# A transformer block on one core: the first batch's ranking and maxima beside products, the last batch's second half of tokens first, the next batch's turned tiles in the last group of heads

## The chip, the core and the metric

One core of one Trainium2 chip runs the whole kernel. The metric is the device time of one execution in microseconds (us).

## What is computed

Eight batches (B = 8) of 1024 tokens with 512 features go through three sublayers. `ln` is a layer norm without weights.

```python
def ffn(y):                       # expert-choice routing, 75% of the tokens
    scores = y @ w_router
    top = top_k(scores, 768)      # per batch
    y[top] = gelu(y[top] @ w_block)
    return y
x = x + 0.5 * ffn(ln(x))
h = ln(x)                         # 16 heads of 32, latent width 64, causal
q_lat = (h @ Wq.T) per head @ q_to_latent;  k_lat = h @ Wk_down.T;  v_lat = h @ Wv_down.T
x = x + (softmax(mask(q_lat @ k_lat.T / 8)) @ v_lat @ v_up) @ Wout.T
x = x + 0.5 * ffn(ln(x))
```

## The kernel before, in words

**Events.** `program_order()` (line 100) returns one list of events for the whole kernel. Each engine's program walks this list and emits its own share of every event, so the list is the order of the work on every engine, and on SyncE (SP), which issues the DMAs. Nothing is reordered later: an engine that waits holds up all that follows it. Every product of matrices is made of three passes of high and low parts (`passes`, line 721), so that most results are copied twice: the high part by ScalarE (ACT), the low part, result minus high, by VectorE (DVE).

The events are, with the engines that take part:

- XL, XR, XS, OUT: 1 MB loads, reloads, spills and stores of half a batch of x (SP).
- ST, VA, RS, NM: statistics of a tile of 128 tokens (DVE), variance, its power -0.5 (GpSimd, POOL), scaled mean. NO: the normalized tile (ACT, two slots).
- T: four transposes of a normalized tile (TensorE, PE), high part (ACT), low part (DVE). The first index is 0 for the first feed-forward layer, 1 for attention, 2 for the last layer.
- SD, SM, SC, RT, RF: the ranking of the tokens. SD is the dot product with the router (DVE), SC a row of scores (PE, ACT), RT compares one tile's scores with all 1024 (DVE, two or three instructions), RF makes the selection.
- GX, F, G, CB: scaling of x (POOL), block product (PE), gelu (ACT), the sum into x (DVE).
- LAT, Q, K, V: the projections. WS: splitting a weight into high and low (ACT, DVE).
- S, MX: scores of a unit of 512 columns for two heads, less the row maximum; and the product that finds the row maxima of the next group of four heads (PE, then exp on ACT for S, reductions on DVE for MX). MC, XT: gather and transpose the maxima (DVE, PE), and a DMA of the row (SP, line 570).
- AM: causal mask (POOL). PV, DEN: products with values and with ones (PE). AC, HT, HR, HE: division of the heads (ACT, DVE).
- HS: a quarter of the heads split for the output product (ACT high, POOL low). O: the output product of a tile (PE) and its sum into x (DVE).

**Stages.** Heads come in four groups (g = 0 to 3) of four. `attention(b)` (line 173) gives each group 18 chunks, two for each of the 9 units: chunk 2u holds the first pair of S and MX, chunk 2u + 1 the second. Beside the scores of group g run the maxima of group g + 1, so group 3 has no maxima; there both S pairs of a unit stand in chunk 2u. PV and DEN come two units behind. Into these chunks other work is put: the end of the batch before into group 0, the next batch's statistics into group 1, its eight T of layer 0 with NO into group 2 (lines 265 to 268), its dots, SC, RT, RF, GX and first two F into group 3 (lines 269 to 277). `project(b, left)` (line 134) then holds the other F, the projections and the first maxima of the next batch, and `back(b)` (line 217) the output products and most of the last feed-forward layer.

**First and last batch.** For batch 0, `front(0)` and `project(0, None)` run alone: ranking comes after all weights but one are split (line 140), most maxima stand in `project`, and units 5 and 6 of the maxima with XT stand alone behind it (line 249). For batch 7, the split of the heads (HS) follows all of attention (line 282); then come O in the order of the tiles, and RT, GX, CB and the store.

**PSUM.** `take(ring, first, size, count)` (line 315) gives each result its banks from rings that are walked in the order of the list; a result waits until the last user of its bank is copied away. S and MX beside each other take four banks of ring A (0 to 5); T of layer 0 in later batches takes one bank of the same ring (line 331); group 3's S take ring N (0 to 3); SC and the first F ring F (4 and 5); PV and DEN have banks 6 and 7. The projections and the early maxima share ring H, all eight banks.

Of the kernel before, what the change touches and what calls it, by code (L numbers as in the profile page):

```python
# [99 lines left out]
def program_order():  # L100


    def stats(s, b, i):
# [9 lines left out]
    def front(b):  # L113


        out = []
        for c in range(NC):
            for i in range(TC * c, TC * (c + 1)):
                out += stats(0, b, i)
            out += scales(0, b, c)  # L120
        out += [("NO", 0, b, 0), ("NO", 0, b, 1)]
        for i in range(NT):
# [94 lines left out]
    def back(b):  # L217


        def more(kind, *rest):  # L220
# [831 lines left out]
```

## Time and profile before

| what | value |
|---|---|
| median of 3 runs | 2492.73 us (2490.47 to 2492.91) |
| the profiled execution's own time | 2491.35 us |
| its span | 2489.6 us |
| PE / DVE / ACT / POOL busy | 90% / 73% / 47% / 16% |
| TensorE clock granted, mean | 0.963 of full speed |

The span runs from the first instruction to the last. The share of busy time is a mean over stages: one batch takes about 300 us, and eight of them overlap only in part. Granted clock is 1.00 at 2.4 GHz and 0.50 at 1.2 GHz.

### The profile page before, as it was taken

The page shows a single profiled execution, that of the slowest core. Times are in us where ns is not written, and L with a number is a line of the kernel's source. Part 1 is how long each engine was busy: PE and PEld are TensorE (multiplying, and loading weights), DVE is VectorE, ACT ScalarE, POOL GpSimd, SP SyncE. Part 2 cuts the span into 40 slices and gives each one's busy share as a digit, 9 for nine tenths or more (in the row PEclk, how much of TensorE's full clock was granted, in tenths as well). Part 3 has the DMA queues.
Part 4 walks back from the last instruction along what each step waited for, and adds up shares of the span by engine and source line. Part 5 has one row for each costly group of instructions (what it writes and reads, how often), then busy time and mean ns, then how long its engine had stood idle before and what let it go on. Part 6 is the DMA issues. An engine that isn't in the chain of part 4 may idle for free.

```text
span 2489.6 us, 53117 instructions
## 1 busy us (share of the span) xinstructions
PE 2253.0 (90%) x21504; PEld 1395.5 (56%) x21504; DVE 1807.2 (73%) x5077; ACT 1181.1 (47%) x2070; POOL 395.8 (16%) x510
## 2 busy tenths in 40 slices
PE   5779999999998999999999999989998899988976
PEld 4534477445674556644566446754476445764445
DVE  5668757887678766787667876778757787678726
ACT  3335543465434654446434464345643455434542
POOL 0101211112101121011111102111111112111121
PEclk9879999899999999999999999989999999999988
DMA  3200021100301002010021101120021100301000
GB/s 131 102 1 3 2 84 53 69 2 6 98 35 69 3 19 85 35 69 3 20 83 52 53 2 53 52 74 29 2 78 59 69 3 2 95 8 69 2 2 34
DMA packets 69601, 106.42 MB, mean 43 GB/s; under 512 B 2544, under 2 KB 32752, under 8 KB 67312
## 3 DMA queue, kind: packets, MB, share of 16 engines
q1 hardware_dynamic: 69360, 103.03, 12.2%
q8 instruction: 173, 2.83, 0.5%
q14 instruction: 68, 0.56, 0.1%
HBM read 64.75 MB, written 37.75 MB: 41 GB/s over the span
## 4 chain that ended last, share of the span: by engine, by line
PE 71%; DVE 15%; issue 6%; ACT 6%; POOL 2%; DMA 0%; DVEq 0%; POOLq 0%; ACTq 0%
PE psum L726 27%; PE psum L739 18%; PE psum L839 9%; PE psum L846 7%; DVE psum L984 4%; PE psum L742 4%; ACT pr L706 4%; DVE part L982 3%; PE psum L768 2%; PE psum L753 2%; DVE junk L932 1%; DVE junk L934 1%; DVE nt_l L907 1%; POOL x L604 1%; ACT nt_h L625 1%
## 5 line engine op out<-in xcount | busy, mean ns | idle before, releaser
L706 ACT ACTIVATE pr<-psum 128x512 f32<-128x512 f32 x1152 | 617.7, 596 | 607.3 <-PE psum L742 607.2
L739 PE MATMUL psum<-qk,qk 32*128 32x512 f32 (+3 forms) x4608 | 519.3, 373 | 95.5 <-DVE part L984 41.7
L984 DVE CUSTOM_DVE_ANT_0 psum<-psum,mask_b 128x512 f32<-128x512 f32 (+3 forms) x1024 | 472.4, 521 | 115.9 <-PE psum L753 114.2
L739 PEld LDWEIGHTS psum<-qk,qk 32*128 32x128 f32 x4608 | 326.4, 190 | 403.6 <-DVE part L984 124.2
L753 PE MATMUL psum<-qk,qk 32*128 32x512 f32 (+3 forms) x4608 | 520.5, 376 | 25.5 <-DVE part L982 19.7
L982 DVE TENSOR_REDUCE part<-psum 128x1 f32<-128x512 f32 x512 | 324.8, 680 | 45.9 <-PE psum L753 43.8
L753 PEld LDWEIGHTS psum<-qk,qk 32*128 32x128 f32 x4608 | 318.5, 191 | 50.1 <-DVE part L982 26.1
L839 PE MATMUL psum<-pr,v_sb 128*32 128x512 f32 (+3 forms) x3072 | 316.6, 508 | 1.6 <-ACT ht L625 1.6
L617 POOL TENSOR_SCALAR_AFFINE_SELECT pr<-pr 128x512 f32<-128x512 f32 x256 | 159.2, 641 | 962.2 <-ACT pr L706 962.2
L846 PE MATMUL psum<-pr,ones 128*32 128x512 f32 (+3 forms) x3072 | 312.0, 501 | 0.0
L646 ACT ACTIVATE norm<-x,nmr,rstd 128x512 f32<-128x512 f32 x192 | 152.4, 811 | 173.0 <-DVE nmr L901 173.0
L742 PE MATMUL psum<-mrow,minus 1*128 1x512 f32 (+3 forms) x1536 | 218.5, 349 | 0.0
L907 DVE TENSOR_TENSOR nt_l<-psum,nt_h 128x512 fp32r<-128x512 f32 x192 | 131.0, 686 | 109.3 <-ACT nt_h L625 107.9
L726 PE MATMUL psum<-wb_h,nt_h 128*128 128x512 f32 x512 | 206.9, 404 | 1.8 <-ACT nt_act L670 1.8
L726 PE MATMUL psum<-wb_h,nt_l 128*128 128x512 f32 x512 | 200.6, 392 | 0.0
L726 PE MATMUL psum<-wb_l,nt_h 128*128 128x512 f32 x512 | 200.4, 391 | 0.0
L768 PE MATMUL psum<-ident,norm 128*128 128x128 f32 x768 | 122.7, 288 | 41.3 <-ACT norm L646 31.5
L604 POOL TENSOR_SCALAR x<-x,gain,shift 128x512 f32<-128x512 f32 x128 | 104.7, 837 | 338.6 <-DVE gain L949 338.6
L625 ACT ACTIVATE nt_h<-psum 128x512 fp32r<-128x512 f32 x192 | 114.6, 597 | 84.5 <-PE psum L768 84.4
L846 PEld LDWEIGHTS psum<-pr,ones 128*32 128x32 f32 x3072 | 77.3, 109 | 121.5 <-issue 105.6
L768 PEld LDWEIGHTS psum<-ident,norm 128*128 128x128 f32 x768 | 89.4, 145 | 99.7 <-issue 46.0
L984 DVE DVE_READ_ACCUMULATOR2_ANT part<- 128x1 f32 x1024 | 143.5, 140 | 0.0
(109 smaller groups left out, 3277.6 us busy)
## 6 DMA issues: line engine op xcount, KB each, us to landing
x<-x_dram SPq DMA_DIRECT2D x16, 1024.0 KB, 6.7
spill_x<-x SPq DMA_DIRECT2D x16, 1024.0 KB, 4.7
x<-spill_x SPq DMA_DIRECT2D x16, 1024.0 KB, 7.3
out_dram<-x SPq DMA_DIRECT2D x16, 1024.0 KB, 5.0
w_h<-scratch_o SPq DMA_DIRECT2D x28, 256.0 KB, 3.1
w_l<-scratch_o SPq DMA_DIRECT2D x28, 256.0 KB, 3.3
w_h<-scratch_q SPq DMA_DIRECT2D x6, 1024.0 KB, 4.9
w_l<-scratch_q SPq DMA_DIRECT2D x6, 1024.0 KB, 7.1
```

The lines of the kernel that those rows point to most:

```text
L617: nc.gpsimd.affine_select(out=tri, in_=tri, compare_op=ALU.is_ge, fill=0.0, base=0, pattern=[[0, HQ], [1, P]], channel_multiplier=-1).then ...
L706: nc.scalar.activation(pr_of(b, g, u)[:, 2 * p + place, :], bank(e, place), ACT.Exp, scale=SCALE).then_inc(exp_ready, 1)
L726: m = eng.matmul(o, a_cols(lhs, k), b_cols(rhs, k), start=(k == 0 and t == 0), stop=(k == n - 1 and t == 2))
L739: eng.matmul(o, (k_h, k_h, k_l)[t][own, P * j:P * (j + 1)], (q_h, q_l, q_h)[t][own, queries], start=(t == 0 and at == 0), stop=False, skip ...
L742: m = eng.matmul(o, minus[row_at:row_at + 1, :].broadcast_to([1, P]), mrow[row_at:row_at + 1, queries], start=False, stop=True, skip_group ...
L753: m = eng.matmul(bank(e, place)[:, at:at + w], (q_h, q_h, q_l)[t][own, P * i:P * (i + 1)], (k_h, k_l, k_h)[t][own, BANK * block:BANK * blo ...
L768: m = eng.transpose(bank(e)[:, n * P:(n + 1) * P], norm[:, slot, n * P:(n + 1) * P], ident[:])
L839: m = eng.matmul(bank(e)[h * DH:(h + 1) * DH, BANK - w:BANK], v_sb[:, j, P * g + DH * h:P * g + DH * (h + 1)], own[:, h, :], start=(j == 0 ...
L846: m = eng.matmul(bank(e)[h * DH:(h + 1) * DH, BANK - w:BANK], ones[:], own[:, h, :], start=(j == 0), stop=(j == LAST_TILE[c]), skip_group_ ...
L907: nc.vector.tensor_tensor(low[:, i, :, :], bank(e).rearrange("p (k t) -> p k t", k=NK), high[:, i, :, :].bitcast(F32), ALU.subtract).then_ ...
L982: m = nc.vector.tensor_reduce(top_of, scores, AX_X, ALU.max)
L984: m = nc.vector.tensor_tensor_reduce(scores, scores, mask_b[:, BANK - w:BANK], 1.0, FAR, ALU.add, ALU.max, top_of)
```

## The change

1. `opening()` replaces `front(0)` and `project(0, None)`: SC of the first half comes after tile 5, each of the first four F is followed by two RT, the splits of weights 1 to 3 stand after the fourth RT, K is put ahead of Q where maxima need it, and eight of the nine maxima units stand between projections. The last K of groups 2 and 3 follow behind XT. All early maxima of batch 0 take ring H.
2. In every batch but the last, T of the next batch moves from group 2 to group 3 with its NO, into ring F.
3. In the last batch six of the eight HS stand in chunks 5, 7, ... 15 of group 3, and `closing()` replaces `back(7)` and `ending(7)`: tiles 4 to 7 first in O, T, the dots and GX. The last stores are cut in two each.

```diff
+    def opening():
...
+            out += scales(0, 0, c)
+        out += [("NO", 0, 0, 0), ("NO", 0, 0, 1)]
         for i in range(NT):
-            out += [("T", 0, b, i)] + ([("NO", 0, b, i + 2)] if i + 2 < NT else [])
-            out += dot(0, b, i) + ([("SC", 0, b, i // TC)] if i % TC == TC - 1 else [])
-            out += [("WS", 0)] if i == TC else []
-        return out
...
+            out += [("T", 0, 0, i)] + ([("NO", 0, 0, i + 2)] if i + 2 < NT else []) + dot(0, 0, i)
+            out += [("WS", 0)] if i == TC else [("SC", 0, 0, 0)] if i == 5 else []
+        out += [("SC", 0, 0, 1)]
+        for i in range(TC):
+            out += layer(0, 0, i) + [("RT", 0, 0, 2 * i), ("RT", 0, 0, 2 * i + 1)]
+            out += [("WS", 1), ("WS", 2), ("WS", 3)] if i == 1 else []
+        out += [("RF", 0, 0)] + [("GX", 0, 0, i) for i in range(NT)]
+        out += layer(0, 0, 4) + layer(0, 0, 5) + summed(0, 0) + summed(0, 1)
+        out += layer(0, 0, 6) + summed(0, 2) + summed(0, 3) + scales(1, 0, 0) + [("WS", 4)] + layer(0, 0, 7)
+        out += [("NO", 1, 0, 0), ("NO", 1, 0, 1)]
+        after = [summed(0, 4), summed(0, 5), summed(0, 6), summed(0, 7) + scales(1, 0, 1)]
+        for i in range(TC):
+            out += [("T", 1, 0, i)] + ([("NO", 1, 0, i + 2)] if i + 2 < TC else []) + after[i]
+        out += [("LAT", 0, 0), ("XS", 0, 0), ("NO", 1, 0, 4), ("NO", 1, 0, 5), ("K", 0, 0, 0)]
+        out += [("Q", 0, 0, 0), ("T", 1, 0, 4), ("NO", 1, 0, 6), ("T", 1, 0, 5), ("NO", 1, 0, 7)]
+        out += [("Q", 0, 1, 0), ("T", 1, 0, 6), ("T", 1, 0, 7)] + maxima(0, 0, 7) + [("LAT", 0, 1), ("XS", 0, 1)]
+        out += [("XL", 1, 0), ("XL", 1, 1), ("K", 0, 0, 1), ("Q", 0, 0, 1)]
+        beside = [[("Q", 0, 1, 1)], [("K", 0, 1, 0), ("K", 0, 1, 1)], [("V", 0, 0), ("V", 0, 1)], [("Q", 0, 2, 0)],
+                  [("Q", 0, 2, 1)], [("Q", 0, 3, 0)], [("Q", 0, 3, 1)], [("V", 0, 2), ("V", 0, 3), ("V", 0, 4)]]
+        for u, rest in zip((0, 1, 2, 3, 4, 5, 6, 8), beside):
+            out += maxima(0, 0, u) + rest + sum([gathered(0, 0, c) for c in range(NC) if LAST[c] == u], [])
+            out += turned(0, 0, 1) if u == 8 else []
+        out += [("V", 0, 5), ("V", 0, 6), ("V", 0, 7), ("K", 0, 2, 0), ("K", 0, 2, 1)] + turned(0, 0, 0)
+        return out + [("K", 0, 3, 0), ("K", 0, 3, 1)]
...
-        out = [] if b else [("F", 0, b, 0), ("F", 0, b, 1)]
-        out += [("G", 0, b, 0), ("G", 0, b, 1)]
-        out += [] if b else [("WS", 1), ("WS", 2), ("WS", 3)] + [("RT", 0, b, i) for i in range(NT)] + [("RF", 0, b)]
-        out += [] if b else [("GX", 0, b, i) for i in range(NT)]
+        out = [("G", 0, b, 0), ("G", 0, b, 1)]
...
-        out += layer(0, b, 4) + summed(b, 2) + summed(b, 3) + scales(1, b, 0) + ([] if b else [("WS", 4)])
...
-        out += [("XR", b - 1, 0), ("XR", b - 1, 1)] if b else [("XL", 1, 0), ("XL", 1, 1)]
-        splits = [[("HS", b - 1, g, c)] if b else [] for c in range(NC) for g in range(NQ)]
+        out += [("XR", b - 1, 0), ("XR", b - 1, 1)]
+        splits = [[("HS", b - 1, g, c)] for c in range(NC) for g in range(NQ)]
         keys = [[("K", b, n // NC, n % NC)] for n in range(NT)]
-        loads = [[("W2", b - 1, "o", g)] if b else [] for g in range(NQ)]
+        loads = [[("W2", b - 1, "o", g)] for g in range(NQ)]
         out += [("Q", b, 0, 1)] + loads[0] + keys[1] + [("V", b, 0)] + splits[0] + [("V", b, 1)] + splits[1]
         out += [("Q", b, 1, 1)] + loads[1] + maxima(b, 0, 0) + splits[2] + [("Q", b, 2, 1)] + loads[2] + maxima(b, 0, 1) + splits[3]
...
-        if b + 1 == B:
-            out += [("RT", 1, b, i) for i in range(2, NT)] + layer(1, b, 6) + layer(1, b, 7)
...
+    def closing(b, left):
+        out = left[0] + [("HS", b, NQ - 1, 1)] + left[1] + left[2] + left[3] + [("HS", b, NQ - 1, 0)]
+        def added(i):
+            return [("O", b, i)] + stats(2, b, i)
+        def turn(i):
+            after = (i + 2) % NT
+            return [("T", 2, b, i)] + ([("NO", 2, b, after)] if i % TC < 2 else [])
+        for i in range(TC, NT):
+            out += added(i)
+        out += scales(2, b, 1) + [("NO", 2, b, 4), ("NO", 2, b, 5)] + added(0) + added(1) + turn(4)
+        out += added(2) + turn(5) + dot(1, b, 4) + added(3) + turn(6) + dot(1, b, 5) + scales(2, b, 0) + turn(7) + dot(1, b, 6)
+        out += dot(1, b, 7) + [("SC", 1, b, 1), ("NO", 2, b, 0), ("NO", 2, b, 1)] + layer(1, b, 4) + turn(0) + dot(1, b, 0)
+        out += turn(1) + dot(1, b, 1) + dot(1, b, 2) + dot(1, b, 3) + layer(1, b, 5) + [("SC", 1, b, 0)] + turn(2) + turn(3)
+        out += [("RT", 1, b, i) for i in range(NT)] + [("RF", 1, b)]
+        order = (4, 5, 6, 7, 0, 1, 2, 3)
+        out += [("GX", 1, b, i) for i in order]
+        for i in (6, 7, 0, 1, 2, 3):
+            out += layer(1, b, i)
+        for i in order:
+            out += [("CB", 1, b, i)] + ([("OUT", b, i // TC)] if i % TC == TC - 1 else [])
...
-    sched = [("XL", 0, 0), ("XL", 0, 1)] + front(0) + project(0, None)
-    sched += maxima(0, 0, 5) + maxima(0, 0, 6) + sum([gathered(0, 0, c) + turned(0, 0, c) for c in (1, 0)], [])
+    sched = [("XL", 0, 0), ("XL", 0, 1)] + opening()
...
-            groups[1] = [weave(groups[1], ahead, 0, len(groups[1]))] + [[("NO", 0, b + 1, 0), ("NO", 0, b + 1, 1)]]
+            groups[1] = [weave(groups[1], ahead, 0, len(groups[1]))]
+            groups[2] += [[("NO", 0, b + 1, 0), ("NO", 0, b + 1, 1)]]
+            chunks = groups[3]
             for u in range(NT):
-                groups[2][2 * u] += [("T", 0, b + 1, u)]
-                groups[2][2 * u + 1] += [("NO", 0, b + 1, u + 2)] if u + 2 < NT else []
-            chunks = groups[3]
+                chunks[2 * u] += [("T", 0, b + 1, u)]
+                chunks[2 * u + 1] += [("NO", 0, b + 1, u + 2)] if u + 2 < NT else []
...
             chunks[17] += [("F", 0, b + 1, 1)]
+        else:
+            for n, (g, c) in enumerate((g, 1 - c) for g in range(NQ - 1) for c in range(NC)):
+                groups[NQ - 1][2 * n + 5] += [("HS", b, g, c)]
         sched += sum(sum(groups, []), [])
         if b + 1 < B:
             sched += project(b + 1, left) + back(b)
         else:
-            sched += sum(left, []) + [("HS", b, g, c) for c in range(NC) for g in range(NQ)] + back(b) + sum(ending(b), [])
+            sched += closing(b, left)
...
-            early = k == "MX" and e[2] == 0 and e[3] not in (5, 6)
+            early = k == "MX" and e[2] == 0 and (e[3] not in (5, 6) or e[1] == 0)
...
-        elif k == "T" and e[1] == 0 and e[2] > 0:
-            own = banks[e] = take("A", 0, 6, 1)
-        elif (k == "SC" or k == "F" and e[3] < 2) and e[1] == 0 and e[2] > 0:
+        elif (k in ("T", "SC") or k == "F" and e[3] < 2) and e[1] == 0 and e[2] > 0:
             own = banks[e] = take("F", 4, 2, 1)
...
+                    if b + 1 == B:
+                        sp.wait_ge(x1_ready, x1_nth["CB", 1, b, TC * c + 1])
+                        eng.dma_start(out[b, rows(c), :].rearrange("(i p) e -> p i e", p=P)[:, 0:2, :],
+                                      x1[:, TC * c:TC * c + 2, :]).then_inc(x_out[c], 16)
                     sp.wait_ge(x1_ready, x1_nth["CB", 1, b, TC * c + TC - 1])
-                    eng.dma_start(out[b, rows(c), :].rearrange("(i p) e -> p i e", p=P), x1[:, TC * c:TC * (c + 1), :]
-                                  ).then_inc(x_out[c], 16)
...
+                        eng.dma_start(tiles, x1[:, TC * c:TC * (c + 1), :]).then_inc(x_out[c], 16)
+                    else:
+                        eng.dma_start(tiles[:, 2:TC, :], x1[:, TC * c + 2:TC * (c + 1), :]).then_inc(x_out[c], 16)
...
-                        act.wait_ge(hsl_ready, nth["HS", b, NQ - 1, NC - 1])
+                        act.wait_ge(hsl_ready, max(nth["HS", b, NQ - 1, c] for c in range(NC)))
...
-                    act.wait_ge(heads_ready, nth["HE", b, NQ - 1, 0])
-                    act.wait_ge(q_done, nth["Q", min(b + 1, B - 1), NQ - 1, c])
+                    if b + 1 < B:
+                        act.wait_ge(heads_ready, nth["HE", b, NQ - 1, 0])
+                        act.wait_ge(q_done, nth["Q", b + 1, NQ - 1, c])
+                    else:
+                        act.wait_ge(heads_ready, nth["HE", b, g, c])
+                        act.wait_ge(s_done, nth["S", b, 1, UNITS - 1, 1])
...
-                    dve.wait_ge(scol_ready, nth["SM", f, b, NC - 1])
-                    dve.wait_ge(srow_ready, nth["SC", f, b, NC - 1])
+                    dve.wait_ge(scol_ready, max(nth["SM", f, b, c] for c in range(NC)))
+                    dve.wait_ge(srow_ready, max(nth["SC", f, b, c] for c in range(NC)))
```

## Rows read from the trace of the kernel before

**Rows 1.** Windows: time, busy us (instructions) per engine, PEclk, DMA share, GB/s

```profile
60.00:70.00 10.00, 0.00 (x0) 0.00 (x0) 8.74 (x20) 0.00 (x0) 7.33 (x8) 0.54 0.00 0
...
150.00:160.00 10.00, 7.67 (x56) 4.37 (x55) 4.51 (x8) 3.49 (x7) 0.00 (x0) 0.50 0.00 0
...
2410.00:2420.00 10.00, 3.35 (x8) 2.67 (x9) 0.81 (x2) 4.26 (x8) 8.34 (x7) 0.62 0.00 0
```

**Rows 2.** Timeline of SP, third and last batch: start us, us, the maxima's DMA

```profile
785.91 0.55 SPq L570 DMA_DIRECT2D mrow<-mxt  x1
826.70 0.53 SPq L570 DMA_DIRECT2D mrow<-mxt  x1
873.23 0.53 SPq L570 DMA_DIRECT2D mrow<-mxt  x1
...
2324.49 0.53 SPq L570 DMA_DIRECT2D mrow<-mxt  x1
2364.90 0.53 SPq L570 DMA_DIRECT2D mrow<-mxt  x1
```

**Rows 3.** Timeline of DVE and ACT, first batch up to the ranking

```profile
23.07 0.69 DVE L907 TENSOR_TENSOR nt_l<-psum,nt_h 128x512 fp32r<-128x512 f32 x1 [2.69 <-ACT nt_h L625]
25.57 2.29 DVE L881 TENSOR_TENSOR wb_l<-raw_b,wb_h 128x2048 fp32r<-128x2048 f32 x1 [1.14 <-ACT wb_h L625]
33.14 0.60 ACT L625 ACTIVATE srow<-psum 128x512 f32<-128x512 f32 x1 [4.55 <-PE psum L774]
47.94 1.27 DVE L934 TENSOR_SCALAR_CACHE_REDUCE junk<-srow,scol 128x1024 bf16<-128x1024 f32 x1
62.40 0.17 DVE L949 TENSOR_SCALAR gain<-gain 128x8 f32<-128x8 f32 x1
```

**Rows 4.** Timeline of PE and DVE, first batch, projections to the first scores

```profile
80.82 0.77 PE L726 MATMUL psum<-nt_h,wlat_h 128*128 128x512 f32 x1 [2.75 <-DVE nt_l L907]
86.24 0.69 DVE L961 TENSOR_TENSOR lat_l<-psum,lat_h 128x512 fp32r<-128x512 f32 x1 [2.28 <-ACT lat_h L625]
117.57 2.47 DVE L982 TENSOR_REDUCE part<-psum 128x1 f32<-128x512 f32 x4
138.05 1.66 PE L753 MATMUL psum<-qk,qk 32*128 32x256 f32 x24 [3.34 <-DVE part L984]
146.24 0.79 PE L739 MATMUL psum<-qk,qk 32*128 32x512 f32 x2 [1.77 <-DVE mxt L999]
```

**Rows 5.** Chain of waits: start us, us; one Q, first batch; last DEN and four O, last batch

```profile
92.49 2.79 PE psum L726 x12
...
2407.44 0.91 PE psum L846 x16
...
2416.66 14.02 PE psum L726 x48
```

**Rows 6.** Timeline of PE, third batch, group 2: one T

```profile
849.21 0.66 PE L768 MATMUL psum<-ident,norm 128*128 128x128 f32 x4
```

**Rows 7.** Timeline of PE and ACT, third batch, group 3

```profile
893.14 0.97 PE L739 MATMUL psum<-qk,qk 32*128 32x512 f32 x12 [0.40 <-ACT pr L706]
896.58 1.09 PE L739 MATMUL psum<-qk,qk 32*128 32x384 f32 x24 [0.39 <-ACT pr L706]
894.37 2.06 ACT L706 ACTIVATE pr<-psum 128x512 f32<-128x512 f32 x4 [1.38 <-PE psum L742]
```

**Rows 8.** Timeline of POOL and DVE, last batch's end

```profile
2411.66 9.88 POOL L611 TENSOR_TENSOR nt_l<-ht,nt_h 128x512 fp32r<-128x512 f32 x8 [8.82 <-ACT nt_h L625]
2460.03 1.28 DVE L934 TENSOR_SCALAR_CACHE_REDUCE junk<-srow,scol 128x1024 bf16<-128x1024 f32 x1 [2.77 <-ACT srow L625]
2474.50 0.17 DVE L949 TENSOR_SCALAR gain<-gain 128x8 f32<-128x8 f32 x1
2482.96 1.84 DVE L955 SCALAR_TENSOR_TENSOR x<-act_b,sel,x 128x512 f32<-128x512 f32 x2 [0.58 <-POOL x L604]
```

**Rows 9.** DMA issues of the page: count, KB each, us to landing

```profile
out_dram<-x SPq DMA_DIRECT2D x16, 1024.0 KB, 5.0
```

More of the change, by code:

```diff
@@ L111, in dot @@
         return [("SD", f, b, i)] + ([("SM", f, b, i // TC)] if i % TC == TC - 1 else [])
[L113 to L122, printed above, removed]
-            out += [("T", 0, b, i)] + ([("NO", 0, b, i + 2)] if i + 2 < NT else [])
-            out += dot(0, b, i) + ([("SC", 0, b, i // TC)] if i % TC == TC - 1 else [])
-            out += [("WS", 0)] if i == TC else []
-        return out
     def layer(f, b, i):
@@ L132, in summed @@
         return [("CB", 0, b, i)] + stats(1, b, i)
+    def opening():
+        out = []
+        for c in range(NC):
+            for i in range(TC * c, TC * (c + 1)):
+                out += stats(0, 0, i)
+            out += scales(0, 0, c)
+        out += [("NO", 0, 0, 0), ("NO", 0, 0, 1)]
+        for i in range(NT):
+            out += [("T", 0, 0, i)] + ([("NO", 0, 0, i + 2)] if i + 2 < NT else []) + dot(0, 0, i)
[22 more added lines that the diff above has]
+        return out + [("K", 0, 3, 0), ("K", 0, 3, 1)]
@@ L134, in project @@
     def project(b, left):
-        out = [] if b else [("F", 0, b, 0), ("F", 0, b, 1)]
-        out += [("G", 0, b, 0), ("G", 0, b, 1)]
-        out += [] if b else [("WS", 1), ("WS", 2), ("WS", 3)] + [("RT", 0, b, i) for i in range(NT)] + [("RF", 0, b)]
-        out += [] if b else [("GX", 0, b, i) for i in range(NT)]
+        out = [("G", 0, b, 0), ("G", 0, b, 1)]
         out += layer(0, b, 2) + layer(0, b, 3) + summed(b, 0) + summed(b, 1)
-        out += layer(0, b, 4) + summed(b, 2) + summed(b, 3) + scales(1, b, 0) + ([] if b else [("WS", 4)])
+        out += layer(0, b, 4) + summed(b, 2) + summed(b, 3) + scales(1, b, 0)
@@ L147, in project @@
         for i in range(TC):
-            out += [("T", 1, b, i)] + ([("NO", 1, b, i + 2)] if i + 2 < TC else []) + (left[i] if left else []) + after[i]
+            out += [("T", 1, b, i)] + ([("NO", 1, b, i + 2)] if i + 2 < TC else []) + left[i] + after[i]
         out += [("LAT", b, 0), ("XS", b, 0), ("NO", 1, b, 4), ("NO", 1, b, 5)]
@@ L220, in more @@
         def more(kind, *rest):
-            return kind(b + 1, 0, *rest) if b + 1 < B else []
+            return kind(b + 1, 0, *rest)
         def turn(i):
@@ L237, in back @@
         out += layer(1, b, 4) + [("RT", 1, b, 0), ("RT", 1, b, 1)] + layer(1, b, 5)
-        if b + 1 == B:
-            out += [("RT", 1, b, i) for i in range(2, NT)] + layer(1, b, 6) + layer(1, b, 7)
+        return out
+    def closing(b, left):
[18 more added lines that the diff above has]
+            out += [("CB", 1, b, i)] + ([("OUT", b, i // TC)] if i % TC == TC - 1 else [])
         return out
@@ L548, in _ @@
                     b, c = e[1:]
+                    if b + 1 == B:
+                        sp.wait_ge(x1_ready, x1_nth["CB", 1, b, TC * c + 1])
+                        eng.dma_start(out[b, rows(c), :].rearrange("(i p) e -> p i e", p=P)[:, 0:2, :],
+                                      x1[:, TC * c:TC * c + 2, :]).then_inc(x_out[c], 16)
                     sp.wait_ge(x1_ready, x1_nth["CB", 1, b, TC * c + TC - 1])
-                    eng.dma_start(out[b, rows(c), :].rearrange("(i p) e -> p i e", p=P), x1[:, TC * c:TC * (c + 1), :]
-                                  ).then_inc(x_out[c], 16)
+                    tiles = out[b, rows(c), :].rearrange("(i p) e -> p i e", p=P)
+                    if b + 1 < B:
+                        eng.dma_start(tiles, x1[:, TC * c:TC * (c + 1), :]).then_inc(x_out[c], 16)
+                    else:
+                        eng.dma_start(tiles[:, 2:TC, :], x1[:, TC * c + 2:TC * (c + 1), :]).then_inc(x_out[c], 16)
                 elif k == "W2":
@@ L571, in _ @@
             for c in range(NC):
-                sp.wait_ge(x_out[c], 16 * B)
+                sp.wait_ge(x_out[c], 16 * (B + 1))
         @block.gpsimd
@@ L691, in _ @@
                     b, g, c = e[1:]
-                    act.wait_ge(heads_ready, nth["HE", b, NQ - 1, 0])
-                    act.wait_ge(q_done, nth["Q", min(b + 1, B - 1), NQ - 1, c])
+                    if b + 1 < B:
+                        act.wait_ge(heads_ready, nth["HE", b, NQ - 1, 0])
[3 more added lines that the diff above has]
+                        act.wait_ge(s_done, nth["S", b, 1, UNITS - 1, 1])
                     copy(nt_of(2, b)[0][:, TC * c:TC * (c + 1), g, :], heads_of(g, c)).then_inc(hsh_ready, 1)
```

## The prediction

> **What bounds the kernel now.** I read the windows first, for where TensorE (PE) is idle, then the marks between groups of heads, then the timelines of the stretches that the change touches, and last the chain of waits. The kernel is bound by PE on the whole, 90% busy, but not at its two ends. In the first batch PE does nothing from 60 to 70 us, and from 150 to 160 us it works at half clock, 0.50 granted. Near the end it is busy 3.35 us of 10 [rows 1]. Between the ends the maxima's DMA marks the groups: group 1 of the third batch takes 826.70 - 785.91 = 40.8 us, group 2 873.23 - 826.70 = 46.5 us. The last batch's group 2, which has no T, takes 2364.90 - 2324.49 = 40.4 us [rows 2]. So three independent stretches are changed: the opening, the groups 2 and 3 of seven batches, and the closing. The sum is made against the profiled execution's own 2491.35 us; the median of the runs is 1.4 us above it.
>
> **Opening, up to the first layer's end.** SC of the first half no longer stands ahead of T of tile 4, so DVE does not sit idle 2.69 us before that tile's low part, nor 1.14 us before the low part of weight 0 [rows 3]: -3.8 us to the last score row. Before, RT began 47.94 - 33.14 - 0.60 = 14.2 us after that row, since three weight splits and the first two gelus stand ahead of it on ACT and DVE. Now four tiles of RT come at once, while PE makes F. All of RT and RF takes 62.57 - 47.94 = 14.6 us [rows 3]. By my reading of the list: row ready at 29.8, four RT to 36.5, splits (which wait for gelu 1 and for one another, as before) to 44.4, four RT and RF to 52.3. That is 10.3 us before 62.6. GX, CB, the statistics and T of attention follow as before, with the 2.29 us split of the last weight where it was, so LAT starts at 80.8 - 10.3 = 70.5. PE's products themselves end only 3.8 us earlier; what shrinks is the idle time behind them, by 6.5 us to some 9 (PE idle all through the first window of [rows 1]), still long enough for the clock to fall (0.54 in that window), so I leave LAT at half speed.
>
> **Opening, projections to the first scores.** Before: 146.24 - 80.82 = 65.4 us [rows 4]. After, on PE: LAT of the first half at half clock 86.24 - 0.60 - 80.82 = 4.8 us [rows 4]; LAT and eight Q at 2.72 us, 12 matmuls (2.79 with the start [rows 5]), 24.5; 16 K and V of three matmuls, 0.68 each, 10.9, less 0.7 where a K runs beside a V; four T at 0.59, 2.4; nine maxima units, 0.95 each and 0.1 more for three with two segments, 8.9; XT 0.4. Sum 51.2. To that come waits. K right behind its LAT waits for the high and the low copy, 1.3 us (0.60 + 0.69 [rows 3]), twice; the first maxima unit waits the same for the Q right ahead of it; LAT of the second half 0.4 for the last T. DVE needs 2.47 us for a unit of maxima and 0.6 for each low part [rows 4], so between units 1 and 3, which have only K and V beside them, PE waits some 2.2 us for banks of ring H. After unit 8 the last K waits for a bank that XT holds until the row's DMA is done, and the first S for that K's low part, some 2.6 us more. Waits 9.1, in all 60.3: -5.1 us. The 3.34 us and like waits for units 5 and 6 by themselves [rows 4] are what this replaces. DVE's own sum in the stretch is nine units (24 us) and 22 low parts (13 us), 37 us, so it does not bound as a whole. The SP queue: spill, load and row DMA keep their order, and the load's wait for NO ends 20 us before the first row DMA. Opening: -10.3 - 5.1 = **-15.4 us**.
>
> **The clock in the first scores.** With nothing from PV yet, half a unit takes 2.85 us at half clock (five of them from 146.24 on), PE busy 7.67 of 10 us, and the clock stayed at 0.50 all the while [rows 1, 4]. At full clock I get 1.9 us each and 1.7 us less for the first PV and the next S: at most -6 us. I take 0, because PE has some 1.4 us of work in the last 3.4 us before the first S, and is then idle 40% of the loop. The Trainium skill ("TensorE: Matmul & The Clock Gate", Part 1) has the clock as a gate that opens by activity and closes again by itself; were the now denser projections to keep it open, the sum would be the -6 us one, and no row shows such a start at 1.00.
>
> **Groups 2 and 3, seven batches.** In group 2 a T costs (46.5 - 40.4) / 8 = 0.76 us [rows 2]. Without its eight T the group should take the last batch's 40.4 to group 1's 40.8, and with group 1's extra DVE work not there I take 40.6: -5.9 us. In group 3 a unit takes 896.58 - 893.14 = 3.44 us, bound by a loop of S, four exps and S again, in which PE waits 0.40 us [rows 7]. A T costs PE 0.59 us (its 0.66 less the overlap [rows 6]). Where PE waits, 0.4 is covered and 0.1 to 0.2 stays; where it doesn't (units 0 and 7, and 1 and 2 with their SC) all stays: 4 x 0.59 + 4 x 0.13 = 2.9. ACT has a gap of 1.38 us in each unit [rows 7], and gets a high part and a NO, 1.2 us: covered, but in unit 1, with SC and AC too, about 0.2 over. DVE now meets T low parts ahead of the dots and waits there for ACT, so the second SC comes late by 0.7. I add 0.2 for ring F, where T and SC alternate over two banks: +4.0. RT and RF, 14.6 us of DVE work [rows 3], stretch and end some 5 us later against the group. Behind them GX (8 us on POOL) and two masks; CB needs a gelu that ACT can start only after the last exp, and PV of unit 7 comes behind six F (16 us), so both stay covered. If that cover were gone, each us of RF would be one of PE. Moving the first two NO from group 1's end to group 2's end costs 0: ACT has 1.6 us there. Net -5.9 + 4.0 = -1.9, by seven: **-13 us**. Bounds: +2.4 us if only the uncovered four count, and +5.9, what T cost in group 2: -24 to 0.
>
> **Closing.** Before, PE waits for HS until 2416.66; the POOL halves take 9.88 / 8 = 1.24 us each [rows 5, 8]. Six HS now lie in group 3 of the last batch, one high copy per unit on ACT (0.6 of its 1.38 gap) and one low on POOL behind a mask, 2.5 of 3.4 us: cost 0. HS of the second half is done before the last DEN ends at 2408.4 [rows 5], so O starts 8.3 us earlier and at full clock (four O took 14.02 us [rows 5], 10.9 at full clock): 11.4 us won on PE. Not all of it reaches the end. The dots of tiles 4 to 7 and the statistics of tiles 0 to 3 must pass DVE before SC, and PE is then out of work from about 2432.5 to 2438. I expect the clock to fall there, as after the same idle before [rows 1], costing 2.5 us on F of tile 4. Through F, T 0 and 1, F, dots 0 to 3, SC and T 2 and 3 I get RT from 2452.0 instead of 2460.03 [rows 8]: -8.0. RT, RF, GX and CB keep their pace (2474.50 to 2484.80 [rows 8]); the other six F end under them. The last store is half as large: 5.0 us for 1 MB [rows 9], of which I take 1.3 off (nothing to 2.5, the half). **-9.3 us**; bounds -6 (PE at half clock longer) and -12 (no fall).
>
> **Sum.** 2491.35 - 15.4 - 13 - 9.3 = 2453.6, and 1.4 more for the median: 2455.
>
> **Rivals.**
> A. Group 3 gives back all: units there grow by T's 0.76 us as in group 2. For: the loop has only 0.40 us to spare. Against: that spare exists, and group 2 also had T in the ring of S. Time 2455 + 13 = 2468. Chance 0.15.
> B. The clock stays up: at 1.00 in the first scores (-6) and in the closing gap (-2.5). Against: the rows above. 2455 - 8.5 = 2446.5. With it stands that group 3 absorbs T better, down to 2444 with half of its bound. Chance 0.15.
> C. Slower: in group 3 DVE takes two RT (3.4 us) ahead of every T low part from tile 3 on; should PE wait for those, since ring F has two banks, five waits of 3.4 us come to 17 us a batch: 2455 + 7 x (17 - 4) = 2546. It decides from (2492.7 - 2455) / 7 + 4 = 9.4 us per batch on. For: DVE has 4.05 us of work in units of 3.56. Against: PE has two units' time until it needs the bank, and the lag grows 0.5 us a unit. Chance 0.03.
> D. The ends bring nothing because their waits were only renamed (K, XT and bank waits in the opening, dots in the closing) and A holds too: within 0.2% of 2492.7. Against: two idle stretches of over 8 us lose their stated cause. Chance 0.02.
> E. The forecast, 0.65.
>
> **Range and chances.** E with its bounds reaches from 2440 to 2470; A lies in it and B too. I give 2438 to 2470. A measurement of this kernel tells about 0.2% (5 us) from no change; A, B and E lie 24 us or more below: faster 0.94; within 0.2% 0.03, slower 0.03.
>
> **What would show it.** First S at 131 us (right: 128 to 134), and RF's gain at 52; group 2 at 40.4 to 41 us by the DMA marks, S to S in group 3 at 3.5 to 3.6 us in units 3 to 6; O from 2408 less the earlier gains, RT 8 us earlier against the end of PV. Wrong would be: T low parts that end waits of PE in group 3, a group 2 above 43 us, PE idle over 4 us between maxima units, or a group 3 of the last batch that grows with HS.

## The result and the profile after

The changed kernel takes 2464.24 us (median of 4 runs, 2460.70 to 2468.05) against 2492.01 us before (4 runs, 2490.47 to 2492.91). The ratio is 0.9888, 95% interval 0.9874 to 0.9903: 27.8 us faster, where 37.7 us were predicted. The time lies in the predicted range of 2438 to 2470 us, but nearer to rival A's 2468 than to the forecast's 2455: the time alone does not tell the two apart, the parts do. Of all executions reported below, one of the kernel with filled waits took 6290 us, and it is left out of that kernel's time.

The profiled execution took 2468.05 us, its span is 2466.3 us and its mean granted clock 0.966. It is 23.3 us below the profiled one of before, and the split below is made against that difference. The page's own line after:

```profile
span 2466.3 us, 53118 instructions
```

The maxima's DMA at the start of each batch's group 1 cuts the span into three parts, as in the prediction:

| part | before | after | measured | predicted |
|---|---|---|---|---|
| start to batch 0's mark | 186.46 | 180.05 | -6.4 | -15.4 |
| batch 0's mark to batch 7's | 2097.65 | 2087.84 | -9.8 | -13 |
| batch 7's mark to the end | 205.5 | 198.4 | -7.1 | -9.3 |

**Opening.** The first layer came out as forecast. GX on POOL, which RF's gain releases, starts 10.1 us earlier (62.67 before, predicted -10.3), and LAT starts at 71.39 instead of 80.82 [rows 4], -9.4 us. But from LAT to the first S it took 68.4 us, more than the 65.4 of before [rows 4], where I had forecast 60.3. The timeline of PE in the changed kernel (start us, us, instruction, idle time before it and what ended it):

```profile
71.39 0.77 PE L783 MATMUL psum<-nt_h,wlat_h 128*128 128x512 f32 x1 [3.68 <-DVE nt_l L964]
...
77.62 0.47 PE L783 MATMUL psum<-lat_h,wkv_h 64*128 64x512 f32 x1 [1.50 <-DVE lat_l L1018]
...
89.44 0.47 PE L783 MATMUL psum<-nt_h,wlat_h 128*128 128x512 f32 x1 [0.93 <-DVE nt_l L964]
...
93.93 0.46 PE L783 MATMUL psum<-lat_h,wkv_h 64*128 64x512 f32 x1 [1.50 <-DVE lat_l L1018]
...
100.90 0.97 PE L810 MATMUL psum<-qk,qk 32*128 32x512 f32 x12 [1.50 <-DVE qk L1023]
...
108.11 0.97 PE L810 MATMUL psum<-qk,qk 32*128 32x512 f32 x12 [0.81 <-DVE part L1039]
...
111.70 0.97 PE L810 MATMUL psum<-qk,qk 32*128 32x512 f32 x12 [1.03 <-DVE part L1039]
...
139.75 0.61 PE L796 MATMUL psum<-qk,qk 32*128 32x512 f32 x2 [1.46 <-DVE qk L1028]
```

The waits are where they were expected, the three behind a product just made at 1.50 us where I had 1.3. What had not been expected stands in the windows of the same stretch (columns as in [rows 1]; the third number from the end is the granted clock):

```profile
80.00:90.00 10.00, 9.07 (x53) 7.12 (x52) 4.58 (x9) 4.55 (x8) 0.00 (x0) 0.90 0.35 117
90.00:100.00 10.00, 7.89 (x26) 5.41 (x24) 3.28 (x8) 1.77 (x3) 0.00 (x0) 0.83 0.06 24
...
110.00:120.00 10.00, 8.97 (x48) 6.20 (x48) 6.76 (x14) 1.79 (x3) 0.00 (x0) 0.83 0.01 2
...
140.00:150.00 10.00, 7.66 (x56) 4.63 (x52) 4.04 (x7) 3.48 (x7) 0.00 (x0) 0.50 0.00 0
```

The granted clock is below 1.00 in three windows in which PE was busy 8 to 9 of 10 us. The chain of waits shows what ran then (start us, us):

```profile
77.62 5.47 PE psum L783 x15
...
93.93 5.48 PE psum L783 x15
...
112.67 4.54 PE psum L783 x12
118.11 2.94 PE psum L783 x12
```

The Q at 112.67 took 4.54 us, the next one 2.94. The two groups of 15 are a K and a Q; the same K and Q at full clock take 3.9 us in the kernel with the first part alone (77.19 to 81.09), so they are 1.6 us too long as well. Three times the clock fell, and three times a Q ran at half clock, for 1.57, 1.57 and 1.60 us more: 4.7 us of the 8.1 that my forecast of the stretch was short by. The falls stand behind the waits at 77.62 and 93.93 and behind the pair at 108.11 and 111.70, where PE waits for banks; behind the third wait of 1.50 us, at 100.90, the window from 100 to 105 us shows 1.00.

**Groups 2 and 3.** SP's timeline, third batch, the marks that open groups 2 and 3 (start us, us), then PE's and DVE's in its group 3, and last PE's in the same group of the kernel before:

```profile
816.16 0.53 SPq L622 DMA_DIRECT2D mrow<-mxt  x1
856.60 0.53 SPq L622 DMA_DIRECT2D mrow<-mxt  x1
```

```profile
861.80 0.97 PE L796 MATMUL psum<-qk,qk 32*128 32x512 f32 x12 [0.94 <-ACT pr L763]
866.48 0.97 PE L796 MATMUL psum<-qk,qk 32*128 32x512 f32 x12
...
871.18 0.98 PE L796 MATMUL psum<-qk,qk 32*128 32x512 f32 x12
...
875.92 0.98 PE L796 MATMUL psum<-qk,qk 32*128 32x512 f32 x12
879.64 0.98 PE L796 MATMUL psum<-qk,qk 32*128 32x512 f32 x12
...
899.97 0.50 PE L783 MATMUL psum<-wb_h,nt_h 128*128 128x512 f32 x1
...
865.68 0.69 DVE L964 TENSOR_TENSOR nt_l<-psum,nt_h 128x512 fp32r<-128x512 f32 x1 [1.89 <-ACT nt_h L677]
...
897.20 0.17 DVE L1006 TENSOR_SCALAR gain<-gain 128x8 f32<-128x8 f32 x1
```

```profile
878.34 0.98 PE L739 MATMUL psum<-qk,qk 32*128 32x512 f32 x12 [0.94 <-ACT pr L706]
...
882.54 0.97 PE L739 MATMUL psum<-qk,qk 32*128 32x512 f32 x12
...
886.12 0.97 PE L739 MATMUL psum<-qk,qk 32*128 32x512 f32 x12
...
911.84 0.50 PE L726 MATMUL psum<-wb_h,nt_h 128*128 128x512 f32 x1
```

Group 2 takes 856.60 - 816.16 = 40.4 us, 6.1 less than the 46.5 of [rows 2], and this in each of the seven batches. Group 3, from its first S to the second F, takes 899.97 - 861.80 = 38.2 us, where before it took 911.84 - 878.34 = 33.5: +4.7 for +4.0 forecast. Units 1 and 2 (4.70 and 4.74 us) are 1.1 us longer than before (886.12 - 882.54 = 3.58) and carry SC besides T; a later one is 0.26 us longer (3.72 against 3.46). Over the seven batches the time from the group 3 mark to the next batch's first mark grows by 30.5 us, 4.4 a batch. In the last batch, from the group 3 mark to the end of the last DEN, it takes 42.3 us against 43.5 before: it does not grow with HS.

**Closing.** PE, DVE and ACT, last batch:

```profile
2421.14 1.08 PE L831 MATMUL psum<-ident,scol 128*128 128x128 f32 x4 [6.16 <-DVE scol L981]
...
2434.27 1.09 PE L831 MATMUL psum<-ident,scol 128*128 128x128 f32 x4 [3.42 <-DVE scol L981]
...
2429.70 0.69 DVE L964 TENSOR_TENSOR nt_l<-psum,nt_h 128x512 fp32r<-128x512 f32 x1 [8.71 <-ACT nt_h L677]
2438.34 1.27 DVE L991 TENSOR_SCALAR_CACHE_REDUCE junk<-srow,scol 128x1024 bf16<-128x1024 f32 x1
...
2427.29 1.28 ACT L722 ACT_TABLE_LOAD   x1 [2.97 <-PE psum L783]
```

The wait for HS ahead of O [rows 5, 8] is gone: O follows the last DEN at once. The last DEN ends at 2391.2, and RT begins 47.1 us later (2438.34); before, that was 2460.03 - 2408.37 = 51.6 us [rows 5, 8]. So 4.5 us were won where I had 8.0. PE has nothing to do for 6.16 us ahead of the first SC (5.5 forecast), and then for 3.42 us ahead of the second, a gap that the prediction does not have. Both SC ran at half clock, 1.08 and 1.09 us. The store ends 3.2 us after the last CB instead of 4.8: -1.6, forecast -1.3.

### The profile page after: what moved, and what is told of

Read it like the earlier page. It is cut to its first block, busy times and chain, and to the rows that moved or that the text cites. A ratio compares the mean times of both kernels' runs of the same rounds, so it can differ in the third digit from the quotient of the medians.

```text
span 2466.3 us, 53118 instructions
## 1 busy us (share of the span) xinstructions
PE 2265.4 (92%) x21504; PEld 1393.1 (56%) x21504; DVE 1814.5 (74%) x5077; ACT 1176.7 (48%) x2070; POOL 396.3 (16%) x510
## 4 chain that ended last, share of the span: by engine, by line
PE 74%; DVE 14%; issue 6%; ACT 5%; POOL 2%; DMA 0%; DVEq 0%; POOLq 0%; ACTq 0%
PE psum L783 28%; PE psum L796 18%; PE psum L896 10%; PE psum L903 9%; PE psum L799 4%; DVE psum L1041 4%; DVE part L1039 3%; ACT pr L763 2%; PE psum L825 2%; PE psum L810 2%; DVE nt_l L964 1%; DVE junk L989 1%; DVE junk L974 1%; DVE junk L991 1%; POOL x L656 1%
## 5 line engine op out<-in xcount | busy, mean ns | idle before, releaser
L677 ACT ACTIVATE qk<-psum 128x512 fp32r<-128x512 f32 x128 | 76.2, 596 | 148.8 <-PE psum L783 148.5
L896 PEld LDWEIGHTS psum<-pr,v_sb 128*32 128x32 f32 x3072 | 71.2, 110 | 130.3 <-issue 101.6
```

Of the source, the lines that this page charges most:

```text
L677: return nc.scalar.activation(dst, src, ACT.Copy)
L896: m = eng.matmul(bank(e)[h * DH:(h + 1) * DH, BANK - w:BANK], v_sb[:, j, P * g + DH * h:P * g + DH * (h + 1)], own[:, h, :], start=(j == 0 ...
```

## The experiments

Each kernel was timed against the one before; the medians and the ratios of those comparisons are given. Four kernels are built on Q ahead of K (0.9854, 0.9839 to 0.9869) with one edit more, and their intervals all overlap with that one: what such an edit is worth rests on its stretch in the trace, one execution each.

**The three parts alone.** Each applies one of the three numbered parts of the change to the kernel before, and leaves the other two.

> The first part of the change alone, in the kernel before. If the three parts add up as in the traces of before and after, the time falls by 6 to 8 us (first S at 140 instead of 146 us), not by the 15.4 us of the prediction. If the predicted sum was right and the later parts took it back, it falls by 13 us or more.

> The second part alone: T of the next batch in group 3. By the marks of after, group 2 falls by 6.1 us and group 3 grows by 4.7: 10 us less over seven batches (range 7 to 13). The rival, that group 3 gives all back, has 0 to 3 us less.

> The third part alone. By the traces 7 us less (range 5 to 9); the prediction had 9.3. From the last DEN's end to the first RT 47 us, with PE idle for 6 us ahead of the first SC and 3.4 us ahead of the second.

| kernel | us | ratio, 95% | gain | predicted |
|---|---|---|---|---|
| opening alone | 2481.30 | 0.9962 (0.9949 to 0.9976) | 9.5 | 15.4 |
| groups alone | 2475.51 | 0.9941 (0.9925 to 0.9956) | 14.7 | 13 |
| closing alone | 2483.70 | 0.9968 (0.9956 to 0.9980) | 8.0 | 9.3 |

The opening and the groups gained more than was expected from the traces (6 to 8 and 7 to 13 us). The product of the three ratios is 0.9871, and 0.9888 was measured with an interval to 0.9874: the parts add up to within the intervals. The groups part is worth what was predicted. The marks of its trace give 2097.65 - 2084.87 = 12.8 us; the 9.8 of the changed kernel is from the slowest of its four executions. So rival A, in which group 3 gives all of it back, is wrong. The opening carries the larger part of the error. Alone it showed the same waits and a granted clock of 0.83 in the windows from 90 and from 110 us, but no fall behind the first wait of 1.50 us:

```profile
77.19 0.47 PE L769 MATMUL psum<-lat_h,wkv_h 64*128 64x512 f32 x1 [1.50 <-DVE lat_l L1004]
...
78.00:80.00 2.00, 2.00 (x9) 1.61 (x9) 0.69 (x1) 0.60 (x1) 0.00 (x0) 1.00 0.74 287
```

So a wait of 1.50 us does not bring the clock down each time: this kernel has two falls in the stretch, the changed one three.

**Q ahead of K.** If the fall of the clock comes from the waits, a product whose inputs are ready should go where PE waits for a copy. Only the order changes:

```diff
-        out += [("LAT", 0, 0), ("XS", 0, 0), ("NO", 1, 0, 4), ("NO", 1, 0, 5), ("K", 0, 0, 0)]
-        out += [("Q", 0, 0, 0), ("T", 1, 0, 4), ...
+        out += [("LAT", 0, 0), ("XS", 0, 0), ("NO", 1, 0, 4), ("NO", 1, 0, 5)]
+        out += [("Q", 0, 0, 0), ("K", 0, 0, 0), ("T", 1, 0, 4), ...
...
-        out += [("XL", 1, 0), ("XL", 1, 1), ("K", 0, 0, 1), ("Q", 0, 0, 1)]
+        out += [("XL", 1, 0), ("XL", 1, 1), ("Q", 0, 0, 1), ("K", 0, 0, 1)]
```

> After, with Q ahead of K behind each LAT of the first batch. Theory: the waits of 1.5 us behind LAT bring the clock down right after (Q at half clock, 1.8 us lost each time), so both waits and both falls go: 5 to 8 us less than after, first S at 132 to 135 us. Rival: the clock falls there whatever stands in front, and only the waits go: 3 to 4 us less. Second rival: the waits move on to later products, 0 to 2 us less.

2454.97 us, ratio 0.9854 (0.9839 to 0.9869): 9.3 us below the changed kernel, more than the 5 to 8 expected. Its windows, its first maxima unit, a later one with the Q up to the next, and its first S:

```profile
80.00:90.00 10.00, 9.07 (x53) 7.12 (x53) 6.91 (x15) 4.36 (x8) 0.00 (x0) 1.00 0.36 118
90.00:100.00 10.00, 8.58 (x54) 5.52 (x53) 6.51 (x11) 2.99 (x5) 0.00 (x0) 1.00 0.00 1
...
110.00:120.00 10.00, 10.00 (x103) 7.70 (x101) 9.18 (x41) 1.80 (x3) 0.00 (x0) 1.00 0.00 0
...
92.78 0.97 PE L810 MATMUL psum<-qk,qk 32*128 32x512 f32 x12 [0.61 <-DVE qk L1023]
...
107.44 0.98 PE L810 MATMUL psum<-qk,qk 32*128 32x512 f32 x12
...
111.30 1.09 PE L810 MATMUL psum<-qk,qk 32*128 32x384 f32 x24
...
130.03 0.79 PE L796 MATMUL psum<-qk,qk 32*128 32x512 f32 x2 [1.46 <-DVE qk L1028]
```

LAT starts at 70.94 and the first S at 130.03: 59.1 us, where the prediction had 60.3 for the order of the change. The clock stays at 1.00 in every window in which it had fallen. PE's waits in the stretch sum to 5.8 us, so its products take 53.3, where the prediction's sum had 51.2: a maxima unit and a Q take 111.30 - 107.44 = 3.86 us at full clock, not 0.95 + 2.72. This swap removes waits and half clock together, so it doesn't say what each is worth. The next pair does.

**Waits filled, order untouched.** Six products of 128x512 into the bank that the waiting product will overwrite, ahead of each K that follows its LAT and ahead of the first maxima unit. Their results are used by nothing.

```diff
+            def filler(o, count):
+                for n in range(count):
+                    eng.matmul(o, wb_h[:, n % NK, 0:P], wb_h[:, n % NK, :], start=True, stop=True, skip_group_check=True)
...
+                    if b == 0 and g == 0:
+                        filler(bank(e), 6)
                     pe.wait_ge(latl_ready, nth["LAT", b, c])
...
+                    if e == ("MX", 0, 0, 0, 0):
+                        filler(bank(e), 6)
```

> After, with the three waits of 1.5 us in the first batch's projections filled: six extra products of the router block's weight with itself (1.3 us at full clock) into the free bank ahead of the wait, before K of group 0 (both halves) and before maxima unit 0. The order is untouched and the real products overwrite the result. Theory that idle time brings the clock down: granted clock 1.00 from 82 to 120 us, each Q 2.72 us, first S 4 to 6 us earlier than in after. Rival that the gain of the swapped order came from the order alone: no gain, or up to 1 us slower.

2459.24 us, ratio 0.9864 (0.9847 to 0.9881). Its stretches are read from a second set of runs of the same kernel:

> The same kernel as fill_waits, for a trace of an undisturbed execution. If idle time brings the clock down: granted clock 1.00 from 82 to 120 us, each Q 2.72 us, K right behind the extra products, first S at 134 to 136 us, against 139.75 in after. If the falls have another cause, they are there again at about 79, 96 and 113 us.

2459.80 us, ratio 0.9875 (0.9859 to 0.9892). Both intervals overlap with the changed kernel's (0.9874 to 0.9903), so the gain is read from the stretch. Its windows, its waits for banks and its first S:

```profile
80.00:90.00 10.00, 9.07 (x57) 7.23 (x56) 6.48 (x14) 4.55 (x8) 0.00 (x0) 1.00 0.32 107
90.00:100.00 10.00, 9.89 (x50) 7.03 (x49) 4.29 (x7) 1.79 (x3) 0.00 (x0) 1.00 0.00 0
...
110.00:120.00 10.00, 10.00 (x91) 7.44 (x89) 8.18 (x29) 1.79 (x3) 0.00 (x0) 1.00 0.00 0
...
104.01 0.97 PE L810 MATMUL psum<-qk,qk 32*128 32x512 f32 x12 [0.81 <-DVE part L1048]
...
107.60 0.97 PE L810 MATMUL psum<-qk,qk 32*128 32x512 f32 x12 [1.03 <-DVE part L1048]
...
134.02 0.79 PE L796 MATMUL psum<-qk,qk 32*128 32x512 f32 x2 [1.46 <-DVE qk L1037]
```

LAT stands at 69.93 and the first S at 134.02: 64.1 us against 68.4. The order is the same and PE has more to do, and yet the stretch is 4.3 us shorter, with the clock at 1.00 from 76 to 130 us, although LAT of the first half takes 0.7 us longer here (5.46 against 4.74). So the half clock behind the waits is shown to cost over 4 us of the 8.1, by itself. The waits for banks of 0.81 and 1.03 us were not filled and are still there, and yet the clock does not fall behind them, nor does it with Q ahead of K: these two waits by themselves do not make the third fall, and what else it takes is not shown. The swap takes 5.0 us more (59.1); the waits that it takes away, 1.50 + 1.50 and 0.89 of the third, are 3.9 of these.

**Fillers in the first scores.** On top of Q ahead of K: eight such products into bank 7 before the first pair of S of batch 0, three before each of the next pairs of units 0 to 2.

```diff
+                if e[0:3] == ("S", 0, 0) and e[3] < 3 and e not in beside_of:
+                    pe.wait_ge(kl_ready, nth["K", 0, 2, 1])
+                    filler(psum[:, 7 * BANK:8 * BANK], 8 if e[3:5] == (0, 0) else 3)
```

> The kernel with Q ahead of K, and in the first five pairs of scores of the first batch three extra products into PV's sister bank (eight ahead of the first pair). If these hold the clock at 1.00, a pair takes 1.9 to 2.1 us instead of 2.85 and the start of group 0 is 4 to 6 us shorter. If the clock falls all the same, each pair gets longer by 0.5 us, 2 to 4 us slower in all.

2451.38 us, ratio 0.9836 (0.9822 to 0.9849), 3.6 us below Q ahead of K alone. First the window with the fillers, then the same one without:

```profile
130.00:140.00 10.00, 10.00 (x83) 6.03 (x85) 5.84 (x9) 5.72 (x10) 0.00 (x0) 1.00 0.00 0
```

```profile
130.00:140.00 10.00, 7.63 (x54) 5.04 (x56) 3.87 (x6) 3.76 (x7) 0.00 (x0) 0.50 0.00 0
```

Group 0's stretch, from the first mark to that of group 1, went from 45.7 to 42.0 us, a little short of the 4 to 6 us expected; the first two pairs of S start at 131.42 and 133.45, 2.0 us apart. Full clock in the first scores is worth 3.7 us here, net of what the fillers take. I had put it at 6 at most, and at nothing for the change as made, which holds: there the clock was 0.50 (the last of the changed kernel's windows above).

**Tail.** On top of Q ahead of K: the last K of groups 2 and 3 ahead of XT of half 0, V5 to V7 behind it.

```diff
-        out += [("V", 0, 5), ("V", 0, 6), ("V", 0, 7), ("K", 0, 2, 0), ("K", 0, 2, 1)] + turned(0, 0, 0)
-        return out + [("K", 0, 3, 0), ("K", 0, 3, 1)]
+        out += [("K", 0, 2, 0), ("K", 0, 2, 1), ("K", 0, 3, 0), ("K", 0, 3, 1)] + turned(0, 0, 0)
+        return out + [("V", 0, 5), ("V", 0, 6), ("V", 0, 7)]
```

> The kernel with Q ahead of K, and the last K of groups 2 and 3 ahead of XT, three V behind it. Theory: the last K's wait for XT's bank (0.98 us) and the first S's wait for that K's low part (1.46 us) go, since V needs only ACT: the first S comes 1.5 to 2.5 us earlier. Rival: XT, and with it the row, comes later and S waits for its DMA: no gain.

2452.33 us, ratio 0.9842 (0.9826 to 0.9859). The interval overlaps most of that of Q ahead of K (0.9839 to 0.9869), so the gain in time isn't shown; in the trace the first S comes 1.2 us earlier (128.81), of which LAT's own start is 1.1 us (69.81 against 70.94), so that the 1.5 to 2.5 us expected of the order are not there. The timeline of its first scores shows something else:

```profile
128.81 0.49 PE L796 MATMUL psum<-qk,qk 32*128 32x512 f32 x2 [0.73 <-ACT v_sb L677]
...
130.78 0.50 PE L796 MATMUL psum<-qk,qk 32*128 32x512 f32 x2 [0.78 <-ACT pr L763]
...
135.22 0.79 PE L796 MATMUL psum<-qk,qk 32*128 32x512 f32 x2 [0.78 <-ACT pr L763]
```

The first pairs of S stand 1.97 us apart at full clock, as the prediction had it (1.9); then the clock falls all the same, and pairs take 2.85 us. Even so the group 1 mark comes 97.0 us after LAT instead of 98.8.

**Dots first.** On top of Q ahead of K: in group 3 the dots stand ahead of T in each chunk, so that DVE does not wait for ACT's high part before a dot whose input is long there.

```diff
             chunks = groups[3]
+            for i in range(NT):
+                chunks[i // 2] += dot(0, b + 1, i)
...
             for i in range(NT):
-                chunks[i // 2] += dot(0, b + 1, i)
```

> The kernel with Q ahead of K, and in group 3 the dots of a chunk ahead of its T, so that DVE makes them while ACT copies the high part. Theory: units 1 and 2 of group 3, 4.7 us each, are held up by the low part ahead of the dots (DVE idle 1.9 us before the first); then group 3 gets 0.5 to 1.2 us shorter, 3 to 8 us in seven batches. Rival: PE and ACT set these units: no change beyond 2 us.

2449.91 us, ratio 0.9826 (0.9811 to 0.9840), 5.1 us below Q ahead of K alone. Units 1 to 3 of the third batch start at

```profile
854.53 0.97 PE L797 MATMUL psum<-qk,qk 32*128 32x512 f32 x12
858.82 0.97 PE L797 MATMUL psum<-qk,qk 32*128 32x512 f32 x12
863.11 0.97 PE L797 MATMUL psum<-qk,qk 32*128 32x512 f32 x12
```

which makes units 1 and 2 each 4.29 us instead of 4.70 and 4.74. Summed over seven batches the time from the group 3 mark to the next batch's first mark shrinks by 5.8 us (1030.5 to 1024.7), near the 5.1 of the medians. So 0.4 of the 1.1 us in units 1 and 2 was DVE held up by the low part of T, as the prediction named it ("the second SC comes late"). The 0.7 us that is left is near the 0.59 of a whole T, uncovered.

**The closing's gaps.** On top of Q ahead of K: F of tiles 4 to 6, whose inputs are ready early, put where PE was idle ahead of the two SC.

```diff
-        out += dot(1, b, 7) + [("SC", 1, b, 1), ("NO", 2, b, 0), ("NO", 2, b, 1)] + layer(1, b, 4) + turn(0) + dot(1, b, 0)
-        out += turn(1) + dot(1, b, 1) + dot(1, b, 2) + dot(1, b, 3) + layer(1, b, 5) + [("SC", 1, b, 0)] + turn(2) + turn(3)
+        out += layer(1, b, 4) + dot(1, b, 7) + [("NO", 2, b, 0), ("NO", 2, b, 1)] + turn(0) + dot(1, b, 0)
+        out += layer(1, b, 5)[:1] + [("SC", 1, b, 1)] + turn(1) + dot(1, b, 1) + dot(1, b, 2) + dot(1, b, 3) + layer(1, b, 5)[1:]
+        out += layer(1, b, 6)[:1] + [("SC", 1, b, 0)] + layer(1, b, 6)[1:] + turn(2) + turn(3)
...
-        for i in (6, 7, 0, 1, 2, 3):
+        for i in (7, 0, 1, 2, 3):
```

> The kernel with Q ahead of K, and in the closing F of tiles 4 and 5 stand where PE waits for the score columns (6.2 us before the first SC, 3.4 us before the second), F of tile 6 in front of the second SC. Theory: PE loses that idle time and the falls of the clock behind it, RT begins 3 to 5 us earlier against the last DEN, and the end with it. Rival: the low part of T of tiles 0 to 3 behind more products comes later, and RT moves by less than 1 us or back.

2451.08 us, ratio 0.9832 (0.9819 to 0.9846), 3.9 us below Q ahead of K alone. The window from 2420 us, with the second SC (2420.48, 0.62 us, behind a wait of 1.32):

```profile
2420.00:2430.00 10.00, 9.22 (x46) 7.70 (x47) 7.45 (x24) 3.27 (x6) 0.00 (x0) 1.00 0.01 2
```

From the last DEN to RT it takes 41.2 us, against 46.7 without this edit: 5.5 us, more than the 3 to 5 expected. The 5.5 us are the gap, its half clock and the order on ACT together. They aren't told apart. It is 2.4 us less than my forecast of the change as it was (51.6 - 8.0 = 43.6).

**All of it.** Q ahead of K, tail, fillers in the first scores (six, then three), dots first and the closing's gaps in one kernel:

> All that gained, together: Q ahead of K, K ahead of XT at the end of the opening, extra products in the first scores, dots ahead of T in group 3, F in the gaps of the closing. Against the kernel with Q ahead of K (2455 us) the parts give 3.6, 1.5, 5 and 4 us, 14 in all if they add: 2441 us, range 2436 to 2446.

2442.25 us (2433.62 to 2443.76), ratio 0.9796 (0.9775 to 0.9816), within the 2436 to 2446 expected of parts that add: 22 us below the changed kernel, and 47.9 below the 2490.19 of before in that comparison.

## Why the prediction was right and wrong

**Right: the direction, that each of the three parts gains, and the size of the groups.** Faster was given 0.94, and the time is inside the range. The first layer (-10.3 forecast, -9.4 measured at LAT), the groups (-13 forecast, -14.7 alone) and the store (-1.3 and -1.6) stand. That the time is inside the range is no proof of the sum: the range also held A, in which the groups give nothing, and both ends came out short. Of the signs named, RF's gain (52.30) and group 2 (40.4) came as said; the first S at 128 to 134 us did not (139.75), nor did the units of 3.5 to 3.6 us in group 3 (3.72).

**Wrong, opening: the step "Sum 51.2. To that come waits."** It took all products from LAT of the second half on at full clock, without a reason given. The waits themselves were listed in the right places, at 1.3 us where they measured 1.50. But the clock fell behind two of the three, and once more behind the two waits for banks, and the Q that followed ran at half: 1.6 us more each time, 4.7 us. The waits in all are 9.7 us, where I had 9.1: 0.6. The rest, 2.8 us, is mostly in the sum itself: with Q ahead of K, where the clock stood at 1.00 from 76 to 125 us, the products took 2.1 us more than 51.2, although LAT of the first half took 0.5 less than its 4.8. The 59.1 us of that kernel point the same way: my sum with its waits would have been about 57. I had named the clock as the risk of the first scores and of the closing, and had not looked for it between two products. Why the clock fell behind some of these waits and not behind others stays open.

**Right on a small point: the clock in the first scores.** I took 0 of the -6 us, and it was 0.50. The Trainium skill ("TensorE: Matmul & The Clock Gate", Part 1), which the prediction weighed here, has the gate opening by activity. The trace with the fillers agrees, at 1.00 with PE busy 10.00 of 10 us, and that was worth 3.7 us in the stretch.

**Nearly right: groups 2 and 3.** Group 2 gave 6.1 us (forecast 5.9), group 3 took 4.7 (forecast 4.0). In the later units the uncovered rest of a T is 0.26 us, where I had 0.13; units 1 and 2 take 1.1 us more each, where I had T whole, 0.59. DVE's lag grew, as said: RF's gain comes 35.4 us after the group's first S, 8.5 us later than before and not 5, and it was still covered. Rival C wanted PE to wait for T's low part in group 3; none of the rows of PE there has such a wait.

**Mechanism right, size off: the closing.** "-8.0" at RT measured -4.5. The gap ahead of SC had the expected length (6.16 us for 5.5) and brought the fall of the clock that I had priced at 2.5. What I had not counted is the second gap of 3.42 us: the high part of T of tile 0 stands on ACT behind a gelu and a table load of 1.28 us (2427.29), so DVE's low part and with it the dots of tiles 0 to 3 come late, and PE has nothing else. SC and T of tiles 2 and 3 then ran at half clock again. Alone, the part gave 8.0 us in time, 1.3 less than forecast.

**The other rivals.** B wanted the clock at 1.00 in the first scores and in the closing gap; it was 0.50, and fell to 0.66 in the window from 2420 us. The fillers and the filled gaps of the closing reach 1.00, by edits of their own. D wanted nothing to be gained at the ends; alone they gave 9.5 and 8.0 us.

**What stays open.** The three parts alone would make 0.9871 x 2492.01 = 2459.9 us, and the changed kernel's median is 4.3 us above that; the intervals allow for it, and no run looked for a cause.

## What to carry to other kernels

When idle time is squeezed out of a stretch, cost the new neighbours: a product that reads the copy of the one right ahead of it waits for both copies, 1.50 us here, and the product behind that wait may run at half clock for another 1.6. Put a product whose inputs are ready into each such place, and where there is none, even a product that nobody reads can pay. Read the granted clock over the stretches that look busy too, and not just over those that look idle.

## What the runs showed that was not expected

- The clock fell to half in a stretch with PE busy 7.89 to 9.07 of 10 us, behind waits of 1.50 us, or of 0.81 and 1.03 us a few us apart. With the same order and the three waits of 1.50 us filled it stayed at 1.00 from 80 to 130 us, the waits for banks among them. Not every such wait did it: behind the third one of 1.50 us, and behind the first one in the kernel with the opening alone, the clock stayed up.
- Work that does nothing made its stretch shorter: 4.3 us for 18 products in the projections (by the medians of the whole kernel 4 to 5 us, with intervals that overlap), 3.7 us for those in the first scores.
- In the first scores PE is busy 7.6 of 10 us at half clock, and the changed kernel's next window is still at 0.65. Started at full clock, the same loop had two pairs at 1.97 us and then dropped to 2.85; with fillers it kept to about 2.0.
